# The sixth PV group of a block moved ahead of the last maxima and output products on TensorE

## The chip, the cores and the metric

One NeuronCore of one Trainium2 chip runs the whole kernel. The metric is the device time of one execution in microseconds (us), and the lower the better.

## What is computed

x has 4 x 2048 tokens of 512 features, the context 4 x 154 tokens. The reference, cut to what matters:

```
x = x + attn(layernorm(x), ctx)          # 16 heads of 32; q from x, k and v from ctx; softmax; @ Wo.T + bo
w = softmax(layernorm(x) @ W_router.T + b_router);  keep the two largest of 8
x = x + sum_e w[e] * (layernorm(x) @ W_experts[e].T + b_experts[e])
```

## The kernel before

The tokens are cut into 16 blocks of 512. The first 880 us or so are attention, router and the scatter of the rows to the experts; the rest is the experts' products, which the change doesn't touch.

In the attention part every engine runs a list of steps written out by hand, one list for each slot (`pe_slot`, `act_slot`, `dve_slot`, `pool_slot`, `sp_slot`), and in a slot it works on several blocks at once: on TensorE, b is the block whose scores are computed, b-1 the one whose output product runs, b+1 the one whose maxima are found and b+2 the one whose queries are made. An engine takes its steps strictly in the order of its list. Steps of different engines are tied by semaphores: a step waits until the one that makes its data, or frees its bank, has counted.

The steps that matter here, with their lines:

- **MX** (L726, `pe_MX`): exact scores of six (token tile, head) pairs, products 0 to 10 of block b+1. They go in turn to two pairs of PSUM banks. VectorE takes the maxima (`dve_DMX`, L975; product 10 has only four pairs and two reductions, L979 and L980) into `mx_sb`.
- **O** (L746, `pe_O`): output product of block b-1 in twelve pieces of four matmuls, three for each tile of 128 tokens. VectorE adds a finished tile to x (`dve_Oe`, L987) and takes its statistics (L566, then L574 when all four are there).
- **PV** (L815 and L818, `pe_PV`): probabilities times values of block b in eight groups, 30 small matmuls each. VectorE normalises after each pair of groups (L1083, L1085). PV4 and PV5 are the pair of the third group of heads. Both wait for the same counts: the lower halves of the probabilities up to product 7, and the normalisation of the second pair.
- **MT** (L756, `pe_MT`): four transposes of the 64 maxima; waits for all eleven maxima steps. ScalarE scales them into `mT` (`act_MTe`, L933), SyncE moves that into the query tile (L1351), where the next slot's scores (**ST**, L786 and L789) need it.
- **LB** (L851, L852, L854, `pe_LB`): 36 very small matmuls, router logits of block b-1. Its bank is the one of the last O tile, so it waits for VectorE's last L987. VectorE's L1006 and L1012 read it; L1012 also waits for a chain over L574, ScalarE's L580 and GpSimd's L597 to L1195.
- **Q6** and the rest (L708, `pe_Q`): query product of block b+2. Q6 uses MT's bank and waits for L933. Q9, in the next slot, uses LB's bank and waits for L1012.
- GpSimd issues the **scatter** of an earlier block (L1252, `scatter`): eight indirect DMAs a block, in two groups of four (`pool_SC`, `pool_SD`), between its other steps.

O products and LB are in a slot only when b-1 is a block (from the third MT on); the scatters run in twelve of the slots that have them.

Of the kernel before, what the change touches and what calls it, by code (L numbers as in the profile page):

```python
# [110 lines left out]
def build(nc, x, ctxT, wqT, bq, wkT, bk, wvT, bv, woT, bo, weT, be, wrT, br, wo, boc, out):  # L111
# [543 lines left out]
    def emptied(step, s):  # L655

        chain = HOLDERS[BANK[step]]
        at = [n for n, _ in chain].index(step)
        for back in range(1, len(chain) + 1):
            name, off = chain[at - back]  # L660
            b = s + (off - (back > at))
            if b.here():
                kind = name.rstrip("0123456789")
                signal, n = EMPTIED[kind]
                if kind == name:
                    return signal, b.at(n, n)
                i = int(name[len(kind):])
                if kind == "ST" and i in PLD:
                    return pldd, b.at(ND, PLD.index(i) + 1)
                return signal, b.at(n, (i // 3 if kind in "QO" else i) + 1)  # L670
        return None
# [9 lines left out]
    def split3(k):  # L681
        return ((0, 0, k), (1, 0, k), (0, 1, k))
# [10 lines left out]
    def pe_Q(e, b, i, s):  # L693

        G, part = i // 3, i % 3
        bank = BANK[f"Q{3 * G}"]
        if b.first and i == 0:
            pe_value(e, 2)
            e.wait_ge(p_bk, 5)
        if i == 0:  # L700
            e.wait_ge(t1e, b.at(4, 4))
        if part == 0:
            if free := emptied(f"Q{i}", s):
                e.wait_ge(*free)
        seqs = [t for k in range(KC) for t in split3(k)]
        for n in range(4 * part, 4 * part + 4):
            wp, xp, k = seqs[n]
            m = e.matmul(W[:, bank, :], wq_s[:, wp, k, G * P:(G + 1) * P], xnT[xp][:, k, :], start=(n == 0), stop=(n == 11))  # L708
        if part == 2:
            m.then_inc(qp, 1)  # L710
        if b.first and i == 11:
            pe_value(e, 3)
            pe_value(e, B)
# [18 lines left out]
    def pe_O(e, b, i, s):  # L732

        j, part = i // 3, i % 3
        bank = BANK[f"O{3 * j}"]
        if b.first and i == 0:
            e.wait_ge(p_bk, 6)
        if i == 0:
            e.wait_ge(ate, b.at(4, 4))
        if part == 0:  # L740
            if free := emptied(f"O{i}", s):
                e.wait_ge(*free)
        seqs = [t for k in range(KC) for t in split3(k)]
        for n in range(4 * part, 4 * part + 4):
            ap, wp, k = seqs[n]
            m = e.matmul(W[:, bank, :], aT[ap][:, k, j * P:(j + 1) * P], wo_s[:, wp, k, :], start=(n == 0), stop=(n == 11))  # L746
        if part == 2:
            m.then_inc(op_, 1)
# [44 lines left out]
    def pe_PV(e, b, w):  # L793

        p, G, q = b.par, w // 2, w % 2
        upto = (5 * G + 4) // 2 + 1
        e.wait_ge(pldp, b.at(NP, sum(n < upto for n in PLP)))
        if any(n < upto for n in PLD):
            e.wait_ge(pldd, b.at(ND, sum(n < upto for n in PLD)))
        if b.first and w == 0:  # L800
            e.wait_ge(p_v, 1)
            e.wait_ge(p_vr0, 64)
        elif w == 0:
            e.wait_ge(ld_v[p], b.half(32, 32))
        if b.first and w == 0:
            e.wait_ge(p_rx, 5)
        if w > 1 or b.past(1):
            e.wait_ge(nmd, b.at(4, G))
        for jj in range(2):
            j = 2 * q + jj  # L810
            tok = slice(j * P, (j + 1) * P)
            o = PVp[:, q, jj * 256:jj * 256 + 132]

            for n, (pp, vv) in enumerate(((0, 0), (0, 1), (1, 0))):
                e.matmul(o, Pst[pp][:, (5 * G + 4) % 10, tok], Vr[p][:, vv, G, :], start=(n == 0), stop=(n == 2))  # L815
            for g in range(4):
                for pp, vv in ((0, 0), (0, 1), (1, 0)):
                    m = e.matmul(o[:, g * 33:(g + 1) * 33], Pst[pp][:, (5 * G + g) % 10, tok], Vm[p][:, 4 * G + g, vv, :],  # L818
                                 start=False, stop=True, skip_group_check=True)
        m.then_inc(pvt, 1)  # L820

    def pe_AT(e, b, G, s):
        e.wait_ge(nmd, b.at(4, G + 1))
        pe_T(e, f"AT{G}", b, s, lambda j, k: att[:, j, 4 * k:4 * k + 4, :].rearrange("p h d -> p (h d)"), G, atp)
# [528 lines left out]
    def pe_slot(e, s):  # L1353
        bm2, bm1, b, bp1, bp2 = s + (-2), s + (-1), s, s + 1, s + 2
        on_bm2, on_bm1, on_b, on_bp1, on_bp2 = bm2.here(), bm1.here(), b.here(), bp1.here(), bp2.here()
        if on_bp1:
            pe_Q(e, bp1, 8, s)
        if on_b:
            pe_ST(e, b, 0, s)
            pe_ST(e, b, 1, s)  # L1360
        if on_bm1:
            pe_PV(e, bm1, 6)
        if on_b:
            pe_ST(e, b, 2, s)
        if on_bp1:
            pe_Q(e, bp1, 9, s)
            pe_Q(e, bp1, 10, s)
            pe_Q(e, bp1, 11, s)
        if on_bm1:
            pe_AT(e, bm1, 0, s)  # L1370
            pe_PV(e, bm1, 7)
        if on_b:
            pe_ST(e, b, 3, s)
        if on_bm1:
            pe_AT(e, bm1, 1, s)
        if on_b:
            pe_ST(e, b, 4, s)
        if on_bp1:
            pe_LA(e, bp1, s)
        if on_bm1:  # L1380
            pe_AT(e, bm1, 2, s)
            pe_AT(e, bm1, 3, s)
        if on_b:
            pe_ST(e, b, 5, s)
            pe_PV(e, b, 0)
            pe_PV(e, b, 1)
        if on_bp2:
            pe_XT(e, bp2, 0, s)
        if on_bm1:
            pe_O(e, bm1, 0, s)  # L1390
            pe_O(e, bm1, 1, s)
        if on_b:
            pe_ST(e, b, 6, s)
        if on_bm1:
            pe_O(e, bm1, 2, s)
        if on_bm2 and not bm2.last:
            pe_R(e, bm2, s)
        if on_b:
            pe_ST(e, b, 7, s)
            pe_PV(e, b, 2)  # L1400
        if on_bp2:
            pe_XT(e, bp2, 1, s)
            pe_XT(e, bp2, 2, s)
        if on_b:
            pe_PV(e, b, 3)
            pe_ST(e, b, 8, s)
            pe_ST(e, b, 9, s)
        if on_bp2:
            pe_XT(e, bp2, 3, s)
        if on_bm1 and not bm1.last:  # L1410
            pe_O(e, bm1, 3, s)
            pe_O(e, bm1, 4, s)
            pe_O(e, bm1, 5, s)
        if on_bp2:
            pe_Q(e, bp2, 0, s)
            pe_Q(e, bp2, 1, s)
        if on_bp1:
            pe_MX(e, bp1, 0, s)
        if on_bp2:
            pe_Q(e, bp2, 2, s)  # L1420
        if on_bp1:
            pe_MX(e, bp1, 1, s)
        if on_bp2:
            pe_Q(e, bp2, 3, s)
        if on_bp1:
            pe_MX(e, bp1, 2, s)
        if on_bp2:
            pe_Q(e, bp2, 4, s)
        if on_bp1:
            pe_MX(e, bp1, 3, s)  # L1430
        if on_bm1 and not bm1.last:
            pe_O(e, bm1, 6, s)
        if on_bp1:
            pe_MX(e, bp1, 4, s)
        if on_bp2:
            pe_Q(e, bp2, 5, s)
        if on_bp1:
            pe_MX(e, bp1, 5, s)
        if on_bm1 and not bm1.last:
            pe_O(e, bm1, 7, s)  # L1440
        if on_bp1:
            pe_MX(e, bp1, 6, s)
        if on_bm1 and not bm1.last:
            pe_O(e, bm1, 8, s)
        if on_bp1:
            pe_MX(e, bp1, 7, s)
        if on_b:
            pe_PV(e, b, 4)
        if on_bp1:
            pe_MX(e, bp1, 8, s)  # L1450
        if on_bm1 and not bm1.last:
            pe_O(e, bm1, 9, s)
        if on_bp1:
            pe_MX(e, bp1, 9, s)
        if on_bm1 and not bm1.last:
            pe_O(e, bm1, 10, s)
        if on_bp1:
            pe_MX(e, bp1, 10, s)
        if on_bm1 and not bm1.last:
            pe_O(e, bm1, 11, s)  # L1460
        if on_b:
            pe_PV(e, b, 5)
        if on_bp1:
            pe_MT(e, bp1, s)
        if on_bm1 and not bm1.last:
            pe_LB(e, bm1, s)
        if on_bp2:
            pe_Q(e, bp2, 6, s)
            pe_Q(e, bp2, 7, s)
# [600 lines left out]
```

## Time and profile before

| | |
|---|---|
| three runs | 1326.05, 1328.01 (median), 1336.47 us |
| profiled execution, its own time | 1329.92 us |
| span in its trace | 1328.2 us |
| TensorE busy | 1213.0 us (91%), 11024 matmuls |
| VectorE, ScalarE, GpSimd busy | 66%, 54%, 56% |
| mean granted TensorE clock | 0.963 of full speed |

The own time of the profiled execution is 1.9 us above the median. Starts in the trace are in us from the first instruction. The end of a matmul is modelled; consecutive matmuls overlap, so the distance between starts is what one takes of TensorE's time. A row of the timeline merges equal instructions, and its second number reaches to the end of the last. What stands in brackets is the engine's idle time ahead of the row and what ended it: "issue" is a wait that the profile can't name, "remote" a signal for which it knows no sender at that moment.

### The profile page before, as it was taken

The numbers are of one execution on the slowest core, as the hardware profiler recorded it, in microseconds if no ns is written. First come the engines' busy times: TensorE is split into PE (matmuls) and PEld (weight loads), VectorE is DVE, ScalarE is ACT, GpSimd is POOL, SyncE is SP. The second block draws the span as 40 slices with busy tenths as digits, with TensorE's granted clock in tenths as the row PEclk, the third lists the DMA queues.
The fourth block names the chain that finished last, engine by engine and source line by source line (L and its number), as shares of the span: only waits on it lengthen the run. The fifth ranks groups of instructions, "written<-read, shape, count | busy, mean of one in ns | idle before, by whom it ended". The sixth has DMA issues, their size and how long they took to land.

```text
span 1328.2 us, 36001 instructions
## 1 busy us (share of the span) xinstructions
PE 1213.0 (91%) x11024; PEld 728.8 (55%) x11025; DVE 880.4 (66%) x1933; ACT 720.3 (54%) x1040; POOL 745.2 (56%) x980
## 2 busy tenths in 40 slices
PE   8987999999989989999998987879899999999997
PEld 4445665665655655655666645534355555555554
DVE  4657787878877878878877877435454555555544
ACT  3436875866775775785686572524243333333333
POOL 4013555665775675676676583755644545444445
PEclk9989998999999999999999998879999999999999
DMA  9842654574583583584575364857989989898886
GB/s 265 258 136 66 175 168 139 174 237 135 172 254 141 149 260 140 151 262 143 163 208 165 109 192 167 324 204 166 210 166 188 180 169 192 175 175 164 166 170 124
DMA packets 117114, 239.22 MB, mean 180 GB/s; under 512 B 18439, under 2 KB 24839, under 8 KB 115847
## 3 DMA queue, kind: packets, MB, share of 16 engines
q1 hardware_dynamic: 84535, 161.24, 40.4%
q0 software_dynamic: 29808, 67.73, 25.1%
q10 hardware_dynamic: 2656, 8.68, 1.8%
q8 instruction: 78, 1.28, 0.4%
q14 instruction: 37, 0.30, 0.1%
HBM read 112.00 MB, written 101.40 MB: 161 GB/s over the span
## 4 chain that ended last, share of the span: by engine, by line
PE 66%; ACT 8%; another core or an unknown queue 7%; DMA 6%; issue 5%; DVE 5%; POOL 1%; SPq 1%; POOLq 1%; ACTq 0%; DVEq 0%
PE S L1855 20%; PE W L708 13%; PE W L746 8%; PE W L678 4%; PE PVp L818 4%; DMA out<-xn,to 4%; PE PVp L1845 3%; PE S L786 3%; ACT xn L620 3%; PE S L726 3%; PE PVp L815 2%; DMA xn<-in_wvT 2%; DVE mx_sb L975 1%; PE S L789 1%
## 5 line engine op out<-in xcount | busy, mean ns | idle before, releaser
L1855 PE MATMUL S<-we_s,wq_s 128*128 x1620 | 376.5, 383 | 12.2 <-DVE wq_s L1811 6.7
L1783 POOL DMA_INDIRECT out<-xn,to x135 | 208.9, 1547 | 211.8 <-DMA out<-xn,to 113.0
L1855 PEld LDWEIGHTS S<-we_s,wq_s 128*128 128x128 f16 x1620 | 158.1, 99 | 180.1 <-issue 21.7
L1172 POOL TENSOR_TENSOR we_s<-P_s,we_s 128x1024 f16<-128x1024 f32 x96 | 203.9, 2136 | 60.7 <-ACT we_s L927 60.4
L1794 ACT ACTIVATE wq_s<-PVp 128x512 f16<-128x512 f32 x137 | 81.6, 597 | 272.6 <-PE PVp L1845 252.2
L1252 POOL DMA_INDIRECT dispatched<-xn,idx x128 | 132.8, 1038 | 91.8 <-ACT xn L620 51.8
L975 DVE TENSOR_REDUCE mx_sb<-S 128x6 f32<-128x924 f32 x160 | 171.3, 1112 | 11.2 <-PE S L726 9.1
L708 PE MATMUL W<-we_s,wq_s 128*128 128x512 f16 x512 | 164.8, 400 | 8.7 <-ACT mT L933 5.3
L746 PE MATMUL W<-wo_s,aT_hi 128*128 128x512 f16 x512 | 166.2, 387 | 2.8 <-DVE aT_lo L953 1.6
L1833 DVE SCALAR_TENSOR_TENSOR att<-S,be_s 128x512 f32<-128x512 f32 x135 | 93.4, 692 | 111.3 <-PE S L1855 100.6
L1811 DVE TENSOR_TENSOR wq_s<-PVp,wq_s 128x512 f16<-128x512 f32 x137 | 94.6, 691 | 36.8 <-ACT wq_s L1794 34.7
L818 PE MATMUL PVp<-Vm,we_s 128*128 128x33 f16 x3072 | 118.6, 179 | 0.3 <-issue 0.3
L927 ACT ACTIVATE we_s<-P_s 128x1024 f16<-128x1024 f32 x96 | 101.8, 1060 | 15.2 <-PE PVp L818 12.1
L726 PE MATMUL S<-Kst,we_s 96*128 96x154 f16 x1024 | 99.6, 233 | 10.9 <-DVE mx_sb L975 5.5
L1091 DVE TENSOR_TENSOR we_s<-S,we_s 128x1024 f16<-128x1024 f32 x64 | 78.1, 1220 | 46.2 <-ACT we_s L927 46.1
L818 PEld LDWEIGHTS PVp<-Vm,we_s 128*128 128x128 f16 x3072 | 106.2, 97 | 0.4 <-issue 0.4
L726 PEld LDWEIGHTS S<-Kst,we_s 96*128 96x128 f16 x1024 | 79.1, 99 | 49.4 <-DVE mx_sb L975 8.0
L870 ACT ACTIVATE we_s<-W,bqs 128x512 f16<-128x512 f32 x64 | 44.0, 689 | 113.7 <-PE W L708 113.2
L708 PE MATMUL W<-xnT_lo,wq_s 128*128 128x512 f16 x256 | 101.8, 398 | 1.7 <-issue 1.7
L909 ACT ACTIVATE P_s<-S 128x1024 f32<-128x1024 f32 x96 | 98.2, 1023 | 8.0 <-issue 4.0
L1801 ACT ACTIVATE xn<-att,wt 128x512 f32<-128x512 f32 x135 | 96.3, 714 | 11.2 <-DVE att L1833 5.2
L746 PE MATMUL W<-wo_s,aT_lo 128*128 128x512 f16 x256 | 99.2, 387 | 0.0
(207 smaller groups left out, 2023.5 us busy)
## 6 DMA issues: line engine op xcount, KB each, us to landing
P_s<-dispatched SPq DMA_DIRECT2D x139, 260.5 KB
we_s<-we_s SPq DMA_DIRECT2D x186, 128.0 KB, 6.1
be_s<-in_x SPq DMA_DIRECT2D x16, 1024.0 KB, 9.9
xR_s<-in_x SPq DMA_DIRECT2D x16, 1024.0 KB
out<-xR_s SPq DMA_DIRECT2D x16, 1024.0 KB
wst<-in_weT SPq DMA_DIRECT2D x16, 512.0 KB, 5.7
we_scratch<-wsp SPq DMA_DIRECT2D x16, 512.0 KB, 5.9
Kst<-k_scratch SPq DMA_DIRECT2D x16, 480.0 KB, 5.1
```

The lines of the kernel that those rows point to most:

```text
L708: m = e.matmul(W[:, bank, :], wq_s[:, wp, k, G * P:(G + 1) * P], xnT[xp][:, k, :], start=(n == 0), stop=(n == 11))
L726: m = e.matmul(S[:, 2 * (BANK[f"MX{n}"] - 2) + u % 6 // 3, (u % 3) * C:(u % 3 + 1) * C], Qst[p][0:96, h, j * P:(j + 1) * P], Kst[p][0:96, ...
L746: m = e.matmul(W[:, bank, :], aT[ap][:, k, j * P:(j + 1) * P], wo_s[:, wp, k, :], start=(n == 0), stop=(n == 11))
L818: m = e.matmul(o[:, g * 33:(g + 1) * 33], Pst[pp][:, (5 * G + g) % 10, tok], Vm[p][:, 4 * G + g, vv, :], start=False, stop=True, skip_grou ...
L909: e.activation(P32[i % R32][:, :, :], at, ACT.Exp, scale=1.0 / (SS * ROOT)).then_inc(exd, 1)
L927: e.activation(Pst[0][:, r:r + 2, :], exps(n), ACT.Copy).then_inc(phd, 1)
L975: e.tensor_reduce(mx_sb[:, 6 * n:6 * n + 6].rearrange("p (a k) -> p a k", a=2), S[:, 2 * h:2 * h + 2, 0:3 * C].rearrange("p a (k c) -> p a ...
L1172: e.tensor_tensor(Pst[1][:, r:r + 2, :], exps(n), Pst[0][:, r:r + 2, :], ALU.subtract).then_inc(pldp, 1)
L1252: e.indirect_dma_start(xs_d.ap(), bass.IndirectOffsetOnAxis(ap=idx[p][:, k * NJ + j:k * NJ + j + 1], axis=0), xn2[p][:, j, :], None).then_ ...
L1783: e.indirect_dma_start(out, bass.IndirectOffsetOnAxis(ap=to[u][:, :], axis=0), yw[u % YW], None, bounds_check=N - 1, oob_is_err=False, com ...
L1801: e.activation(yw[u % YW], yb[u % 2], ACT.Copy, scale=wt[u][:, 0:1]).then_inc(ywd, 1)
L1855: m = e.matmul(Yp[:, u % 2, :], gT[u % 2][xp][:, k, :], we_s[:, bass.ds(n * WN + (wp * KC + k) * D, D)], start=(c == 0), stop=(c == 11))
```

## The change

PV5 is issued one O piece, one MX product and one O piece earlier: O10, PV5, MX10, O11, MT in place of O10, MX10, O11, PV5, MT. Nothing is added or removed, and no other engine's list changes.

```
         if on_bm1 and not bm1.last:
             pe_O(e, bm1, 10, s)
+        if on_b:
+            pe_PV(e, b, 5)
         if on_bp1:
             pe_MX(e, bp1, 10, s)
         if on_bm1 and not bm1.last:
             pe_O(e, bm1, 11, s)
-        if on_b:
-            pe_PV(e, b, 5)
         if on_bp1:
             pe_MT(e, bp1, s)
         if on_bm1 and not bm1.last:
             pe_LB(e, bm1, s)
```

## Rows read from the trace of the kernel before

**Rows 1.** Windows: busy time of PE, PEld, DVE, ACT, POOL, clock, DMA, 300 to 400 us

```profile
300.00:400.00 100.00, 92.24 (x1106) 60.00 (x1103) 80.10 (x170) 70.55 (x99) 67.50 (x102) 1.00 0.60 188
```

**Rows 2.** Timeline of PE, 415 to 421 us: start, length, engine, line, idle before

```profile
415.13 0.43 PE L726 MATMUL S<-Kst,we_s 96*128 96x154 f16 x4
...
416.26 0.34 PE L815 MATMUL PVp<-Vr,we_s 128*128 128x132 f16 x3
...
417.22 0.60 PE L756 MATMUL W<-ident,mx_sb 128*16 128x128 f32 x4
417.65 0.25 PE L851 MATMUL W<-wx_s,aT_hi 128*128 128x16 f16 x4
...
420.00 0.17 PE L854 MATMUL W<-wx_s,aT_lo 128*128 128x8 f16 x1 [0.55 <-issue]
...
420.99 1.03 PE L708 MATMUL W<-we_s,wq_s 128*128 128x512 f16 x2 [0.37 <-ACT mT L933]
```

**Rows 3.** Timeline of DVE, 415 to 419 us

```profile
415.71 0.63 DVE L979 TENSOR_REDUCE mx_sb<-S 128x3 f32<-128x462 f32 x1
416.26 0.31 DVE L980 TENSOR_REDUCE mx_sb<-S 128x1 f32<-128x154 f32 x1
416.48 0.68 DVE L987 SCALAR_TENSOR_TENSOR xR_s<-W,xR_s 128x512 f32<-128x512 f32 x1
...
418.60 0.38 DVE L574 BATCH_NORM_AGGREGATE aggr<-stats 128x2 f32<-128x6 f32 x4 [0.24 <-issue]
```

**Rows 4.** Timeline of ACT, 420 to 421 us

```profile
420.26 0.68 ACT L933 ACTIVATE mT<-W,msh 16x512 f16<-16x512 f32 x1 [6.20 <-remote]
420.84 0.28 ACT L580 ACTIVATE nrm<-aggr,epst 128x4 f32<-128x4 f32 x1
```

**Rows 5.** Timeline of POOL, first scatter beside MT

```profile
414.20 1.08 POOL L1252 DMA_INDIRECT dispatched<-xn,idx  x1 [3.73 <-ACT xn L620]
```

**Rows 6.** Timeline of PE in a slot with LB and no scatter

```profile
173.43 0.43 PE L726 MATMUL S<-Kst,we_s 96*128 96x154 f16 x4
...
175.52 0.60 PE L756 MATMUL W<-ident,mx_sb 128*16 128x128 f32 x4
175.96 0.25 PE L851 MATMUL W<-wx_s,aT_hi 128*128 128x16 f16 x4
...
176.89 0.60 PE L708 MATMUL W<-we_s,wq_s 128*128 128x512 f16 x2
```

**Rows 7.** Timeline of ACT in the same slot

```profile
176.16 0.68 ACT L933 ACTIVATE mT<-W,msh 16x512 f16<-16x512 f32 x1 [6.62 <-PE W L756]
```

**Rows 8.** Line L933: its engine's idle time before it, us, times, by releaser

```profile
  remote: 74.6, 12
  PE W L756: 37.9, 4
```

**Rows 9.** Timeline of POOL: first scatter of the second group, one slot earlier

```profile
375.96 1.08 POOL L1252 DMA_INDIRECT dispatched<-xn,idx  x1 [0.62 <-issue]
```

**Rows 10.** Timeline of PE beside it: PV6, end of ST2, end of Q11

```profile
376.03 0.34 PE L815 MATMUL PVp<-Vr,we_s 128*128 128x132 f16 x3
...
377.39 0.39 PE L786 MATMUL S<-we_s,Kst 97*128 97x512 f16 x1
...
379.99 0.38 PE L708 MATMUL W<-xnT_lo,wq_s 128*128 128x512 f16 x1
```

**Rows 11.** Timeline of ACT beside it: the readers of ST2 and Q11

```profile
380.46 1.02 ACT L909 ACTIVATE P_s<-S 128x1024 f32<-128x1024 f32 x1 [0.77 <-remote]
381.91 0.69 ACT L870 ACTIVATE we_s<-W,bqs 128x512 f16<-128x512 f32 x1 [0.42 <-remote]
```

**Rows 12.** Windows, columns as in Rows 1: behind MT of the shown slot

```profile
420.00:425.00 5.00, 4.63 (x31) 2.06 (x32) 1.80 (x6) 2.48 (x5) 2.08 (x10) 0.66 0.52 194
```

**Rows 13.** Timeline of DVE and of PE, next slot's Q9, a short slot

```profile
327.59 0.69 DVE L1012 SCALAR_TENSOR_TENSOR lg<-lgs,nrm,lgq 128x8 f32<-128x8 f32 x4 [3.16 <-POOL lgq L1195]
...
328.65 0.60 PE L708 MATMUL W<-we_s,wq_s 128*128 128x512 f16 x2
```

More of the change, by code:

```diff
@@ L1456, in pe_slot @@
             pe_O(e, bm1, 10, s)
+        if on_b:
+            pe_PV(e, b, 5)
         if on_bp1:
@@ L1460, in pe_slot @@
             pe_O(e, bm1, 11, s)
-        if on_b:
-            pe_PV(e, b, 5)
         if on_bp1:
```

## Prediction

> **What bounds the kernel now.** I read the windows of the attention part first: in a steady stretch of 100 us TensorE is busy 92.24, VectorE 80.10, ScalarE 70.55 [rows 1]. So a slot, which is some 48 us, is bounded by TensorE, and what counts is its idle time. Then the timeline of TensorE around the place of the change. In the shown slot it runs without a gap through MX10 (415.13), O11, PV5 (416.26), MT (417.22) and the start of LB (417.65), then sits idle in pieces that end at 420.00, named "issue", and again until Q6 at 420.99, which waits for ScalarE's L933 [rows 2]. From the start of MT to Q6 it takes 3.77 us for MT and LB; in a slot without the scatter the same work takes 176.89 - 175.52 = 1.37 us [rows 6]. This is the one big hole of a slot, 2.40 us, and the change is made just in front of it.
>
> What makes the hole? L933 needs MT, which ends at 417.82, but starts at 420.26 [rows 2, 4], 2.44 us late. Where no scatter runs it starts 0.04 us behind MT's end (176.12 to 176.16) [rows 6, 7]. The line's own view has the late kind, "remote", 12 times with 74.6 us, the other 4 times [rows 8]. The first scatter of the group begins at 414.20, before PV5 [rows 5]. The same is seen beside the second group of scatters, at another place: the first begins at 375.96 [rows 9], PV6 is issued at 376.03, ST2's last matmul ends at 377.78, Q11's at 380.37 [rows 10]; their readers start at 380.46 and 381.91, both behind an idle ScalarE that waited for "remote" [rows 11]. So **beside scatters, signals of TensorE reach their readers late after a dense group of small matmuls, and come through at about 4.5 us (380.46 - 375.96) or later behind the first scatter**, while TensorE goes on. If more small matmuls follow at once (PV5, MT, LB are 70), TensorE itself stops as well. That the scatter and the density together do it is read from where it happens; no row shows the mechanism.
>
> By the Trainium skill ("Perfetto Trace Analysis", Tensor Engine Instruction) the end of a matmul in a profile is only estimated, and the signal goes out when PSUM has acknowledged the data. By that alone the small matmuls could simply be slower than drawn, everywhere, and the change would move no time at all; the 0.04 us of the slot without scatter speaks against it.
>
> **The change part by part.** (1) *PV5's own work*: the same 30 matmuls, 417.22 - 416.26 = 0.96 us of TensorE wherever they stand [rows 2]; no instruction is added. PV5 waits for the counts that PV4 has already waited for, so it can't wait in its new place: cost 0. It passes no DMA and no step of another queue. Its reader, VectorE's L1083, is far down VectorE's list, so being earlier is worth 0.
>
> (2) *MX10 and its readers go 0.96 us later.* MX10 ends at 416.52 in place of 415.56. VectorE's two reductions run from 415.71 to 416.57 now, 0.86 us, and L987 follows in 0.59 (to 417.16, it starts 0.09 ahead of the drawn end of L980) [rows 3]. O11 now covers them together with PV5; afterwards O11 alone (0.86) does. Without any late signal: reductions 416.54 to 417.40, MT 0.06 later at 417.46 (now 417.22, +0.24), L987 until 417.99, LB at 418.01 (now 417.65, +0.36). In the two slots with LB and without scatter nothing hides that: there MX10 would end at 173.86 + 0.96 = 174.82, the reductions at 175.70, L987 at 176.29, and Q6 at 176.30 + (176.89 - 175.96) = 177.23 in place of 176.89 [rows 6]. **2 x 0.34 = +0.7 us.** In the earlier slots without LB the reductions are behind VectorE's own queue, 0.
>
> (3) *The twelve slots with scatter.* PV5 now spans 415.13 to 416.09, 0.93 to 1.89 us behind the first scatter, and MX10 follows. That is the situation of PV6 and ST2 (0.07 to 1.82 us behind it) [rows 5, 9, 10]. Upper bound: MX10's signal comes as ST2's did, 4.50 us behind the first scatter, at 418.70. Then the reductions end at 419.56, MT is 419.62 to 420.22, L933 starts at 420.26, exactly as now, because the late signal only sits in front of MT and no longer behind it; L987 ends at 420.15, LB takes 420.17 to 421.10, and with it Q6 at 421.10 in place of 420.99: +0.11. One step better: TensorE's restart in LB at 420.00 lies 0.55 + 0.17 = 0.72 behind the one before [rows 2], and if signals come through in such steps, MX10's may come at 418.00; MT is done at 419.5, LB goes 419.5 to 420.4, Q6 between 420.4 and 420.99: -0.3 in the middle. **12 x 0.11 = +1.3, or 12 x -0.3 = -3.6 us.**
>
> (4) *What is late next.* L987 would end at 420.15, 2.99 later, and everything of VectorE behind it. L574 ends at 418.98 now and ScalarE takes it at 420.84 only, because L933 is ahead of it in its list [rows 3, 4]; with +2.99 it is there at 421.97, and L1012, which hangs on it by way of GpSimd, is 1.1 later. L1012 is done 0.37 before Q9 (328.28, 328.65) in the five short slots (those whose Q6 to Q8 aren't slowed or stopped), so Q9 waits 0.75 there [rows 13]: **5 x 0.75 = +3.8 us** with the later signal; with the earlier one (0.7 less) next to nothing. In the other seven the slack is over 1 us.
>
> Sum with the late signal: 0.7 + 1.3 + 3.8 = +5.8 us; with the earlier one: 0.7 - 3.6 = -2.9 us. The rows of ST2 are nearest to the first, but MX10 is smaller and PV5 begins later beside the scatter than PV6 did, so I take the middle, +1.5. From the profiled execution's own time that is 1329.9 + 1.5 = 1331.4, and less the 1.9 by which it lies above the median, 1329.5; I say **1330 us**, with a range of its own from 1322 to 1338.
>
> **Rivals.** (A) *The hole closes.* The 70 small matmuls are no longer in one piece. If TensorE's traffic is not yet slowed so soon behind the first scatter, and fewer matmuls at once are below what makes it stop, then the values of (2) hold: MT 417.46 to 418.06, L933 at 418.10, Q6 behind LB at 418.94, 2.05 us earlier in each of twelve slots, -24.6 us. The clock would gain as well: behind the hole TensorE runs at half clock in the shown slot (mean 0.66 over five us, about 3.4 us at 1.2 GHz in place of 2.4, or 1.7 us lost) [rows 12], and by the same view in five slots in all, -8.5 us. Together 1298; with half of the hole left 1313. I take 1306. For it: the density is the one thing that PV5, MT and LB share with PV6. Against it: PV6 stood alone and still made its followers late [rows 10, 11].
>
> (B) *A wait in place of a wait, and half clock behind every one.* In (3) TensorE stands idle from 417.22 to 419.62 in one piece, just before MT, where now it has pieces with small matmuls between. If that brings the half clock in all twelve slots, seven more than now, it costs 7 x 1.7 = 12 us on top of the late sum: 1328 + 5.8 + 12 = 1346. The point from which it decides is whether MX10's signal is late at all: if it isn't, the wait is the 0.24 us of (2), and there is none of this. The Trainium skill ("TensorE: Matmul & The Clock Gate", What's actually happening) has a clock gate that goes by how busy the array was and has only the two levels; it speaks against this change in so far as the idle time is gathered in one place, and the half clock behind the hole agrees.
>
> (C) *The change does nothing*, since the hole ends at a fixed time behind the scatter whatever stands in it. That is the forecast's middle and within its range.
>
> **How the numbers follow.** Forecast with (C) 0.60, A 0.27, B 0.13. One per cent, 13 us, is what a measurement of this kernel can tell from no change. A lies below 1314.7 for the most part: faster 0.22. B lies above 1341.3 for the most part: slower 0.10. The rest is 0.68. The range has to reach into A and B: 1304 to 1342, leaving out the lower third of A and most of B's upper half.
>
> **What would show it.** Right: in the slot of 417 us MT starts 2 us or more later than O11 ends, idle by VectorE's L980, L933 still starts about 6 us behind the first scatter, LB runs without "issue" pieces, and Q6 comes within 0.5 us of its place. In the slots without scatter MT is 0.2 and LB 0.3 us later. A would show L933 0.04 us behind MT with Q6 two us sooner; B, half clock in more windows behind MT. Wrong would be, most of all, that dense groups close to the first scatter are not held up, since all of (3) hangs on one neighbouring place.

## The result, and the profile after

The kernel with PV5 in front of MX10 and O11 took 1363.08 us (median of 4 runs, 1358.62 to 1367.85) against 1331.63 us of the kernel before in its 4 runs: **ratio 1.0251, 95% interval 1.0209 to 1.0293**, 2.5% slower. (Ratio and interval are those on record; the quotient of the two medians is 1.0236.) A second measurement (e12 below) gave 1.0215 [1.0174, 1.0257]. The forecast of 1330 us and its range, 1304 to 1342, are missed on the slow side. The profiled execution took 1358.62 us, its span is 1356.9 us, its mean granted clock 0.947 (before: 1329.92, 1328.2, 0.963).

The page's line of busy times and its line of the clock:

```profile
PE 1227.4 (90%) x11024; PEld 731.2 (54%) x11025; DVE 880.4 (65%) x1933; ACT 724.0 (53%) x1040; POOL 746.0 (55%) x980
...
PEclk9989999988988989999989888898999999999999
```

Windows of the changed kernel: the stretch of [rows 1], the whole run of slots, and from MT to ST0 in the slot shown below. Columns as in [rows 1]:

```profile
300.00:400.00 100.00, 90.34 (x987) 57.10 (x986) 74.54 (x153) 62.95 (x88) 59.46 (x95) 0.90 0.49 161
220.00:780.00 560.00, 509.67 (x5855) 324.26 (x5856) 421.60 (x874) 370.31 (x507) 354.06 (x539) 0.93 0.55 173
433.18:439.29 6.11, 6.11 (x53) 3.10 (x54) 4.86 (x13) 2.59 (x5) 1.85 (x9) 0.57 0.42 152
```

The long window of the kernel before, for comparison:

```profile
220.00:780.00 560.00, 519.51 (x6246) 337.77 (x6243) 441.69 (x921) 385.06 (x532) 372.38 (x566) 0.98 0.58 183
```

Fewer instructions fit into the same 560 us on every engine (VectorE 874 for 921), and no engine is busier. TensorE's clock has two levels, so a mean of 0.98 is 22 us at 1.2 GHz out of 560, and 0.93 is 78 us. Behind MT of the shown slot it is 0.57.

The slot of [rows 2] in the changed kernel, TensorE's timeline (PV5, MX10, O11's last piece, MT, LB, Q6):

```profile
427.35 0.34 PE L815 MATMUL PVp<-Vr,we_s 128*128 128x132 f16 x3
...
428.31 0.43 PE L726 MATMUL S<-Kst,we_s 96*128 96x154 f16 x4
...
429.22 0.38 PE L746 MATMUL W<-wo_s,aT_hi 128*128 128x512 f16 x1
433.18 1.02 PE L756 MATMUL W<-ident,mx_sb 128*16 128x128 f32 x4 [3.58 <-DVE mx_sb L980]
433.99 0.30 PE L851 MATMUL W<-wx_s,aT_hi 128*128 128x16 f16 x4
...
435.05 1.04 PE L708 MATMUL W<-we_s,wq_s 128*128 128x512 f16 x2
```

VectorE's timeline of the same slot, to be held against [rows 3]:

```profile
432.26 0.64 DVE L979 TENSOR_REDUCE mx_sb<-S 128x3 f32<-128x462 f32 x1 [4.24 <-remote]
432.81 0.31 DVE L980 TENSOR_REDUCE mx_sb<-S 128x1 f32<-128x154 f32 x1
433.04 0.68 DVE L987 SCALAR_TENSOR_TENSOR xR_s<-W,xR_s 128x512 f32<-128x512 f32 x1
```

ScalarE's L933 there, for [rows 4]:

```profile
434.31 0.68 ACT L933 ACTIVATE mT<-W,msh 16x512 f16<-16x512 f32 x1 [8.03 <-PE W L756]
```

GpSimd's first scatter there, for [rows 5]:

```profile
426.42 1.08 POOL L1252 DMA_INDIRECT dispatched<-xn,idx  x1 [3.71 <-ACT xn L620]
```

PV5 makes MX10's signal late, as the prediction's step (3) had it. MX10 ends at 428.74, yet its reader L979 can't start before 432.26, 3.5 us later. MT (TensorE) has to wait 3.58 us for the reductions. In return L933 starts 0.11 us behind MT's end (434.20), where it was 2.44 us late before [rows 2, 4], and LB runs without an "issue" piece. The late signal has moved from MT to MX10. But it comes 432.26 - 426.42 = 5.84 us behind the first scatter, not 4.50. The line views say the same of all slots. For MT (L756), idle time before it and who waited for it:

```profile
  DVE mx_sb L980: 75.2, 26
...
  ACT mT L933: 126.4, 16
```

The "remote" of [rows 8] is gone from L933; all its 16 waits are for MT itself.

**Where the time went.** Take a slot from the last matmul of MX9 to the next one (414.20 to 463.48 in the slot of [rows 2], 49.28 us). The twelve slots with scatter grew from 49.52 to 52.55 us in the mean: 12 x 3.03 = +36.3. The slots ahead of them and the part behind them are 7.6 us shorter in this execution, which leaves +28.7 of span. Of the 3.03, 1.40 us lie between MX9 and Q6 (6.75 to 8.15), 0.79 between Q6 and ST0 (half clock), 0.84 in the rest. In seven of the twelve MX10's signal came about 5.8 us behind the first scatter, in one 5.1, in four about 4.4. Two slots have LB and no scatter beside it. In the first, MX9 to Q6 takes 0.56 us more (predicted 0.34); the last has no Q6, and MX9 to ST0 takes 0.25 more there.

So two things stand side by side, 2.2 to 3.6 us of TensorE waiting in one piece with half clock behind it, and a VectorE that is 4 us later. By its bookkeeping the first alone could be the cause: over the twelve slots (217.07 to 811.34, now 215.52 to 846.09) the mean clock fell from 0.97 to 0.92, which is some 60 us more at half clock, or 30 us of TensorE's time, of the 36.3. Whether it is has to be tried. The waits of VectorE between 220 and 780 us, largest first, in the changed kernel (total us, times, longest):

```profile
DVE mx_sb L979 <- remote: 41.7, 11, 4.2
DVE xnT_lo L953 <- ACT we_s L862: 20.6, 22, 1.8
DVE we_s L1091 <- ACT we_s L927: 17.5, 17, 1.4
...
DVE lg L1012 <- POOL lgq L1195: 11.5, 8, 1.5
```

and in the kernel before:

```profile
DVE we_s L1091 <- ACT we_s L927: 26.7, 22, 2.9
DVE lg L1012 <- POOL lgq L1195: 24.8, 8, 3.2
DVE xnT_lo L953 <- ACT we_s L862: 18.3, 22, 1.8
```

VectorE idles 20 us more than before in total (560 - 441.69 = 118 us, now 138), with 41.7 of it at a place that had none, and the waits which were its reserve further down (L1091 and L1012 above) have shrunk. Which of the two, TensorE's wait or VectorE's lateness, makes the 33 us is what the last experiments decide.

### The profile page after: what moved, and what is told of

It is laid out like the page before. It is cut to its first block and busy times, and to the rows that moved or that the text cites. A ratio compares the mean times of both kernels' runs of the same rounds, so it can differ in the third digit from the quotient of the medians.

```text
span 1356.9 us, 36001 instructions
## 1 busy us (share of the span) xinstructions
PE 1227.4 (90%) x11024; PEld 731.2 (54%) x11025; DVE 880.4 (65%) x1933; ACT 724.0 (53%) x1040; POOL 746.0 (55%) x980
## 3 DMA queue, kind: packets, MB, share of 16 engines
q0 software_dynamic: 29808, 67.73, 24.6%
## 5 line engine op out<-in xcount | busy, mean ns | idle before, releaser
L708 PE MATMUL W<-we_s,wq_s 128*128 128x512 f16 x512 | 173.2, 418 | 5.2 <-DVE xnT_lo L953 3.4
L746 PE MATMUL W<-wo_s,aT_hi 128*128 128x512 f16 x512 | 163.1, 380 | 3.3 <-DVE aT_lo L953 1.7
L1091 DVE TENSOR_TENSOR we_s<-S,we_s 128x1024 f16<-128x1024 f32 x64 | 78.1, 1221 | 45.4 <-ACT we_s L927 39.1
L597 POOL TENSOR_SCALAR nrm<-aggr 128x4 f32<-128x4 f32 x32 | 7.3, 228 | 180.6 <-ACT nrm L582 180.5
L708 PE MATMUL W<-xnT_lo,wq_s 128*128 128x512 f16 x256 | 105.3, 411 | 0.4 <-issue 0.4
```

## The experiments

Ratios are to the kernel before, measured on the same chip, with their 95% intervals; they are those on record, and the quotient of two medians can differ from them by up to 0.003. "A to Q6" is from MX9's last matmul to Q6, a mean over the twelve slots worked out from the timelines (before 6.75, changed 8.15).

**e1: the change, with the scatters later.** Does the lateness belong to the scatter or to the dense group?

```diff
+        if on_b:
+            pe_PV(e, b, 5)
         if on_bp1:
             pe_MX(e, bp1, 10, s)
         if on_bm1 and not bm1.last:
             pe_O(e, bm1, 11, s)
-        if on_b:
-            pe_PV(e, b, 5)
...
-        if on_bm1 and bm1.here(NB - 3):
-            pool_SC(e, bm1)
         if on_b and not b.last:
             pool_NC(e, b, 1)
             pool_RQ(e, b)
         if on_bm1 and bm1.here(NB - 3):
+            pool_SC(e, bm1)
             pool_SD(e, bm1)
```

> The changed kernel with the first group of four scatters issued with the second group, behind GpSimd's L1195, so that no scatter runs beside PV5, MX10 and MT. If a signal is late because a dense group of small matmuls runs beside scatters: in all twelve slots L756 starts 0.1 to 0.4 us behind O11's end (changed kernel 2.2 to 3.6), L933 0.04 us behind L756's end, and from PV5's start to Q6 it takes 4.0 us as in the slot of 173 us (changed kernel 6.7 to 7.7). If the order alone does it, without the scatter, L756 stays 2.2 us or more behind O11. The whole time isn't forecast, since eight scatters in a row also hold GpSimd's L1172 of the next slot: 1320 to 1375 us.

Measured: 1387.4 us, ratio 1.0479 [1.0427, 1.0531]; the signs are as expected for scatter and density together, the time is 12 us above the wide range given. TensorE's timeline at the place of the change (MT, LB, Q6); the first scatter of this slot begins only at 442.57:

```profile
435.22 0.60 PE L756 MATMUL W<-ident,mx_sb 128*16 128x128 f32 x4
436.00 0.24 PE L851 MATMUL W<-wx_s,aT_hi 128*128 128x16 f16 x4 [0.18 <-DVE xR_s L987]
...
436.90 0.59 PE L708 MATMUL W<-we_s,wq_s 128*128 128x512 f16 x2
```

Without a scatter beside it, the same order of the same matmuls has no late signal: MT follows O11's end (435.13) within 0.09 us and A to Q6 is 4.96 us. The loss has moved to where the scatters now are, to the small matmuls of LA. Waits of TensorE between 220 and 780 us:

```profile
PE W L838 <- issue: 24.3, 33, 1.2
PE W L836 <- issue: 20.8, 36, 1.3
```

The kernel before has 4.0 us of such waits before L836 in its whole span. Scatter and dense group are both needed. LA has 32 small matmuls a slot, and TensorE stops in them for 4.1 us a slot (49.5 us in the twelve, next to nothing before), which costs more than the hole that was closed.

**e2: MX10 first, then PV5, then O11.** It takes away the lateness of MX10 but leaves a dense group ahead of O11's signal.

```diff
             pe_MX(e, bp1, 10, s)
-        if on_bm1 and not bm1.last:
-            pe_O(e, bm1, 11, s)
         if on_b:
             pe_PV(e, b, 5)
+        if on_bm1 and not bm1.last:
+            pe_O(e, bm1, 11, s)
         if on_bp1:
             pe_MT(e, bp1, s)
```

> O10, MX10, PV5, O11, MT: the change without its step past MX10. If what stands behind PV5 is what comes late: MX10's signal is prompt, L979 starts where it did before the change, MT is issued behind O11 without a wait, but O11's signal is late, so the last L987 and with it LB start some 2.5 to 3.3 us later than before the change; Q6 0.5 to 1 us later than before: 1336 to 1346 us, under half of the change's 31. If PV5 ahead of O11 does nothing and only the reductions matter: 1328 to 1334 us. If any shift of PV5 costs the same: 1363 us.

Measured: 1345.32 us, ratio 1.0172 [1.0123, 1.0220]. The signals came as expected and the time lies within 1336 to 1346, but it is 21.5 us above the kernel before on the same chip (1323.79), not under half of the change's loss. TensorE's timeline, MT and LB:

```profile
423.82 0.60 PE L756 MATMUL W<-ident,mx_sb 128*16 128x128 f32 x4
427.40 0.24 PE L851 MATMUL W<-wx_s,aT_hi 128*128 128x16 f16 x4 [2.99 <-DVE xR_s L987]
```

and VectorE's:

```profile
422.31 0.63 DVE L979 TENSOR_REDUCE mx_sb<-S 128x3 f32<-128x462 f32 x1
...
426.56 0.69 DVE L987 SCALAR_TENSOR_TENSOR xR_s<-W,xR_s 128x512 f32<-128x512 f32 x1 [3.40 <-remote]
```

MT is issued without a wait, and most of the loss is still there. What is late is again the first signal behind PV5, here O11's to L987, and with it VectorE.

**e3: the changed kernel with the wait filled.** Twelve products that nobody reads stand in front of MT, so that the clock isn't lost.

```diff
+    def pe_fill(e, s):
...
+        for n in range(FILLS):
+            e.matmul(W[:, bank, :], wq_s[:, 0, n % KC, 0:P], wo_s[:, 0, n % KC, :], start=True, stop=True)
...
+        if on_bp1 and on_bm1 and not bm1.last:
+            pe_fill(e, s)
         if on_bp1:
             pe_MT(e, bp1, s)
```

> The changed kernel with twelve 128x512 matmuls (2.6 us), whose result nobody reads, into MT's bank between O11 and MT, in the slots with O. They fit into the wait of 2.2 to 3.6 us in front of MT, and only keep TensorE busy. If half clock behind an idle stretch is a part of the loss by itself: Q6 to ST0 goes from 3.9 to 4.9 back to 2.6 to 3.0 us in most slots, and the time falls by 10 to 20 us to 1343 to 1353. In the slots without scatter they cost 2.2 us each. If the clock is only a sign and not a cost, or 24 more instructions make the late signal later still: 1360 to 1375.

Measured: 1359.85 us, ratio 1.0275 [1.0219, 1.0332]. The clock came back as expected, the time did not fall to 1343 to 1353; it lies at the lower edge of the rival's range. The window of the run of slots:

```profile
220.00:780.00 560.00, 527.36 (x6096) 339.53 (x6093) 427.65 (x881) 373.57 (x513) 355.32 (x541) 0.97 0.55 174
```

Q6 to ST0 fell from 4.38 to 2.75 us, but the time did not fall. The twelve products also cost 2.0 and 2.3 us in the two slots without scatter, where nothing was idle, so I left the question open here and took it up in e11.

**e4: only half of PV5 moved.** How does the lateness depend on the number of small matmuls?

```diff
+        if on_b:
+            pe_PV(e, b, 5, (0,))
         if on_bp1:
             pe_MX(e, bp1, 10, s)
         if on_bm1 and not bm1.last:
             pe_O(e, bm1, 11, s)
         if on_b:
-            pe_PV(e, b, 5)
+            pe_PV(e, b, 5, (1,))
```

> The changed kernel with PV5's second half (15 of 30 matmuls) moved back behind O11. If the delay grows with how many small matmuls stand in front of the signal: MX10's signal comes 1 to 2 us earlier than in the changed kernel, MT starts 1 to 2 us earlier, 1340 to 1355 us. If any small group there is held until the scatters are over: MT where it is in the changed kernel, 1360 to 1366 us.

Measured: 1318.37 us, ratio 0.9974 [0.9940, 1.0009], much better than the 1340 to 1355 us expected. VectorE's timeline of the slot whose first scatter is at 406.63 (MX10 ends at 408.47):

```profile
409.44 0.64 DVE L980 TENSOR_REDUCE mx_sb<-S 128x3 f32<-128x462 f32 x1 [1.22 <-PE S L726]
```

Behind 15 small matmuls MX10's signal is 1.0 us late, 2.8 us behind the first scatter; behind 30 it is 3.5 late, 5.8 behind it. (So in eight and seven of the twelve slots. In the four where the changed kernel has 4.4, the two are 0.3 and 2.2 us late.) So it is no fixed time behind the scatter, as rival C had it. It grows with what stands in front. A to Q6 is 6.60, and the time is that of before: 1 us more for VectorE costs nothing.

**e5: PV5 beside PV4**, where no scatter runs.

```diff
             pe_PV(e, b, 4)
+            pe_PV(e, b, 5)
...
-        if on_b:
-            pe_PV(e, b, 5)
```

> The kernel before with PV5 directly behind PV4, 3.6 us earlier, so that it is over about 0.6 us before the first scatter begins. If only small matmuls beside scatters delay signals: MX10's signal is prompt, MT starts about 0.2 us later than in the kernel before, L933 within 1 us of MT's end (2.4 before), Q6 0.8 to 2 us earlier in each of twelve slots: 8 to 24 us under the kernel before, ratio 0.982 to 0.994. If instead every move of PV5 ahead of MX10 costs, scatter or not: 1.01 to 1.025.

Measured: 1320.87 us, ratio 0.9941 [0.9914, 0.9968], at the slow edge of what was expected. MX10's signal is prompt (0.04 us in the mean) and L933 starts 0.06 us behind MT. The hole is closed, A to Q6 is 4.01, 1.78 us less once PV5's own 0.96 is set aside, 21 us in twelve slots; 8 us of it arrive. The slot is as long as before (49.53) in the profile, which is of the slowest of its twelve executions (1326.06 us). The largest waits of TensorE between 220 and 780 us:

```profile
PE W L678 <- DVE lga L999: 15.2, 11, 1.9
PE S L786 <- DMA we_s<-mT: 5.1, 6, 1.8
PE W L708 <- issue: 5.0, 1, 5.0
```

TensorE now waits for VectorE's L999 for 15.2 us (10.9 before), for the transfer behind mT (5.1, before 0.9), and in one stop of 5.0. It is ahead, and VectorE isn't.

**e6: PV5 between Q6 and Q7.** The hole closed, PV5 again in a place of its own.

```diff
             pe_Q(e, bp2, 6, s)
+        if on_b:
+            pe_PV(e, b, 5)
+        if on_bp2:
             pe_Q(e, bp2, 7, s)
```

> The kernel before with PV5 behind Q6, so that MT has no dense group ahead of it and LB none beside it but its own. If the backlog of small matmuls makes the delay: MT starts 0.6 us earlier than in the kernel before, L933 within 0.5 us of MT's end, Q6 1.5 to 2.8 us earlier in the twelve slots with scatter, half clock behind it in fewer slots: ratio 0.975 to 0.990. If the delay is tied to the scatter alone, whatever TensorE does: L933 still about 6.0 us behind the first scatter, ratio 0.998 to 1.003.

Measured: 1328.46 us, ratio 1.0015 [0.9983, 1.0047]. The signals came as expected (L933 0.06 us behind MT, 3.1 us behind the first scatter, so not tied to the scatter alone), the gain didn't. A to Q6 is 4.01, but PV5 itself is stopped now:

```profile
PE PVp L818 <- issue: 10.3, 19, 0.8
```

That is only a part of it: TensorE still reaches ST0 1.45 us sooner behind MX9 than before (8.89 for 10.34), while the slot is 0.18 us shorter (49.34).

**e7: MT in front of PV5.** L933's signal is asked for before the dense group.

```diff
-        if on_b:
-            pe_PV(e, b, 5)
         if on_bp1:
             pe_MT(e, bp1, s)
+        if on_b:
+            pe_PV(e, b, 5)
```

> The kernel before with MT in front of PV5 (O11, MT, PV5, LB). If the backlog does it: MT's own signal is prompt (L933 within 0.5 us of MT's end), but PV5 and LB together are 66 dense matmuls and TensorE still stops inside LB until about 5.8 us behind the first scatter; Q6 comes 0 to 0.5 us earlier than in the kernel before: ratio 0.994 to 1.001. If it is the transposes or MT's late signal that stop it: Q6 2 us earlier, ratio 0.98 to 0.985.

Measured: 1323.66 us, ratio 0.9966 [0.9935, 0.9996], as expected. L933 follows MT at once; LB still stands still (TensorE's timeline):

```profile
416.79 0.17 PE L852 MATMUL W<-cb_r,ones 128*128 128x8 f16 x1 [0.54 <-issue]
417.53 0.25 PE L854 MATMUL W<-wx_s,aT_lo 128*128 128x8 f16 x4 [0.58 <-issue]
```

The two restarts lie 417.53 - 416.79 = 0.74 us apart, the step read from [rows 2] too.

**e8: the halves of PV5 behind Q6 and Q7.**

```diff
+        if on_b:
+            pe_PV(e, b, 5, (0,))
+        if on_bp2:
             pe_Q(e, bp2, 7, s)
+        if on_b:
+            pe_PV(e, b, 5, (1,))
```

> As e6, but PV5's first half behind Q6 and its second behind Q7, four large matmuls between. If density is what counts, a little better than e6 (0 to 4 us) or the same; if it is no better or worse, e6's PV5 was no longer delaying anything.

Measured: 1322.48 us, ratio 0.9964 [0.9935, 0.9994], 6.0 us below e6 where 0 to 4 were expected. The stops in PV5 go from e6's 10.3 to 7.5 us, and TensorE's wait for L999 (here L1000) from 6.3 to 12.4.

**e9: one half beside PV4, one behind Q6.**

```diff
             pe_PV(e, b, 4)
+            pe_PV(e, b, 5, (0,))
...
             pe_Q(e, bp2, 6, s)
+        if on_b:
+            pe_PV(e, b, 5, (1,))
+        if on_bp2:
             pe_Q(e, bp2, 7, s)
```

> The kernel before with PV5's first half behind PV4 (before the scatters begin) and its second behind Q6 (no MT or LB beside it). The hole is closed as in e5, e6 and e8 (Q6 4.0 us behind MX9's last matmul, before 6.8), and what is late next is spread: reductions 0 to 0.2 us later, one half of PV5 beside Q6. If the backlog explains all: ratio 0.990 to 0.996, as e5 or better. If what e5 and e8 lost again is set elsewhere in the slot, it is no better than they: 0.994 to 0.998.

Measured: 1321.54 us, ratio 0.9921 [0.9888, 0.9954], as expected. It has the lowest ratio of this study, though its interval overlaps those of e5, e7 and e8, and is faster than the two kernels by about 10 us and 40 us. The waits of TensorE between 220 and 780 us:

```profile
PE W L678 <- DVE lga L1000: 16.0, 12, 1.7
PE W L708 <- issue: 5.2, 1, 5.2
PE W L852 <- issue: 2.1, 12, 0.2
```

Of the "issue" pieces in LB, 18.7 us before, 2.1 are left. The wait for L999 (here L1000) is 5.1 us more, and a single stop in front of a product of Q is 5.2 us instead of 1.7.

**e10: LB behind Q7, PV5 where it was.**

```diff
-        if on_bm1 and not bm1.last:
-            pe_LB(e, bm1, s)
         if on_bp2:
             pe_Q(e, bp2, 6, s)
             pe_Q(e, bp2, 7, s)
+        if on_bm1 and not bm1.last:
+            pe_LB(e, bm1, s)
```

> The kernel before with LB behind Q7, so that PV5 and MT are followed by Q6's large matmuls and nothing dense. If the hole is the lateness of MT's signal (PV5 stands in front of it), L933 still starts about 6 us behind the first scatter, Q6 stays at its place with TensorE idle for all of it and LB comes on top: ratio 1.004 to 1.012. If it is LB that stops TensorE and so keeps MT's signal back: L933 starts within 0.5 us of MT's end, Q6 2.4 us earlier: ratio 0.975 to 0.992.

Measured: 1344.03 us, ratio 1.0088 [1.0058, 1.0118], as expected. TensorE's timeline behind MT (420.79 to 421.39):

```profile
424.54 1.03 PE L708 MATMUL W<-we_s,wq_s 128*128 128x512 f16 x2 [3.16 <-ACT mT L933]
```

With nothing behind MT its signal is as late as before. The lateness comes from what stands in front of MT, and LB only filled it.

**e11 and e12: the fill where it belongs, and the changed kernel beside it.** Ten products, only in the loop's slots and their neighbours:

```diff
-FILLS = 12
+FILLS = 10
...
-        if on_bp1 and on_bm1 and not bm1.last:
+        if on_bp1 and on_bm1 and bm1.here(NB - 3) and not bm1.last:
             pe_fill(e, s)
```

> The changed kernel with ten products (128 x 512, results written over by MT) in front of MT, in the slots of the loop and its neighbours only, so that the slots without scatter have none. They fill 2.1 us of the idle 2.4 to 3.6 us in front of MT. Nothing of the result changes. Theory (the half clock behind MT costs part of the 33 us, and e3's total stood high because its twelve products also lay where nothing was idle, and reached beyond the wait in the slots where it is 2.2 us): half clock between MT and ST0 in none or few of the twelve slots, Q6 to ST0 at 2.6 to 2.8 us in place of 4.38, total 8 to 15 us below the changed kernel, ratio to the kernel before 1.014 to 1.020. Rival (what the clock gives back is taken by the next waits, whatever the fill): total as the changed kernel, ratio 1.023 to 1.029.

> The changed kernel itself, beside e11 on the same chip, as its measure. Both theories: ratio to the kernel before 1.021 to 1.029; MX10's signal 5.8 us behind the first scatter in about eight of the twelve slots and 4.4 in the others, half clock behind MT in all twelve.

Measured: e11 1358.26 us, ratio 1.0285 [1.0253, 1.0318]; e12, the changed kernel, 1349.47 us, ratio 1.0215 [1.0174, 1.0257]. e11's theory (1.014 to 1.020) is missed and its rival (1.023 to 1.029) met; e12's ratio is as expected, but it has half clock behind MT in nine of the twelve slots and not in all. Against what the expectation says, the fills stand in 14 slots, the two without scatter among them. The filled slot from MT to ST0, and the run of slots, in e11's windows:

```profile
426.12:430.30 4.18, 4.10 (x53) 2.38 (x54) 3.91 (x11) 2.44 (x5) 0.77 (x4) 1.00 0.24 91
220.00:780.00 560.00, 526.01 (x6094) 336.71 (x6093) 429.85 (x883) 373.33 (x513) 356.12 (x542) 0.97 0.55 174
```

At full clock this stretch takes 4.18 us, not 6.11. Over the 560 us the half clock falls from 67 us (e12's mean is 0.94) to 34. And the kernel isn't faster for it; it is 0.7% slower, 1.0285 against 1.0215.

That whole time overstates it. The fills in the two slots without scatter make up some 3 us, and behind the twelve slots there is a wait that e12, the changed kernel and the kernel before don't have (e3 has it too), with VectorE idle for 8.51 us in front of it for GpSimd's L1257; whether the fills bring it about was not tried. TensorE's timeline:

```profile
872.25 1.46 PE L795 MATMUL S<-we_s,Kst 97*128 97x512 f16 x3 [7.66 <-DVE we_s L1100]
```

So the slots are the better measure. In the twelve slots TensorE reaches ST0 after 11.05 us instead of 12.11, and the next MX9 after 51.55 instead of 51.82: of the 1.06 us that are won 0.79 are lost again in the same slot, and 0.27, or 3.2 us in twelve slots, are kept. The slot is still 2.03 us longer than in the kernel before. Where the 0.79 goes the waits say; e11 first:

```profile
PE W L679 <- DVE lga L1008: 14.9, 11, 1.8
...
PE W L709 <- DVE lg L1021: 4.1, 8, 0.7
```

and the same two in e12:

```profile
PE W L678 <- DVE lga L999: 9.4, 11, 1.7
...
PE W L708 <- DVE lg L1012: 1.1, 2, 0.7
```

TensorE, sooner at its next steps, waits there for VectorE. Most of the half clock that was taken away lay in time that TensorE had to spare.

**e13 and e14: VectorE alone made later, in the kernel before.** Six or two statistics instructions into a tile that nobody reads; TensorE's list is untouched. They stand behind O11's L988 (the kernel before's L987) and one more statistics instruction, so L988 itself and LB are on time, and all of VectorE's list from there on is later, L575 (L574) included.

```diff
             dve_Oe(e, bm2, 3)
             dve_SN(e, bm2, 2)
+        if on_bm2 and bm2.here(NB - 3) and not bm2.last:
+            for k in range(6):
+                e.bn_stats(dump[:, k, :], wq_s[:, 0, 0, :])
```

> The kernel before, with six statistics instructions of VectorE (128 x 512, into a tile that nobody reads) behind the statistics that follow O11's L987, in the slots of the loop and their neighbours. TensorE's order and signals are as before; nothing of the result changes. At the 0.60 us that one of L566 takes beside the next, VectorE's list is 3.6 us later from there on, about as much as the changed kernel's late signal makes it. Theory (the loss is VectorE's list being 4 us later, of which about 1.6 us a slot are absorbed and the rest is passed on, whatever TensorE's clock does): a slot 1.8 to 2.3 us longer, ratio to the kernel before 1.016 to 1.026, at a granted clock near that of before. Rival (VectorE has 10 us of idle time in a slot and absorbs it; the loss was TensorE's own wait and half clock): ratio 0.998 to 1.006.

> The same with two such instructions, 1.2 us. Theory (the slack comes first, the loss only beyond it): a slot 0 to 0.3 us longer, ratio 0.998 to 1.004. Rival (each us costs the same share, 0.55): a slot 0.7 us longer, ratio 1.006 to 1.009.

Measured: e13 1354.58 us, ratio **1.0264 [1.0241, 1.0288]**; e14 1323.26 us, ratio 1.0034 [1.0009, 1.0058]. e14 is as expected; e13's loss is at the upper end of its theory's 1.016 to 1.026, far from the rival's 0.998 to 1.006, but its clock is not near that of before (0.947, before 0.963). VectorE's timeline of e13, O11's L988 and the added group:

```profile
428.05 0.68 DVE L988 SCALAR_TENSOR_TENSOR xR_s<-W,xR_s 128x512 f32<-128x512 f32 x1
...
429.25 3.64 DVE L1640 BATCH_NORM_STATS2 dump<-wq_s 128x6 f32<-128x512 f16 x6
```

and e13's window of the run of slots:

```profile
220.00:780.00 560.00, 518.52 (x6002) 337.12 (x5998) 469.02 (x951) 375.53 (x516) 357.39 (x542) 0.95 0.56 174
```

3.6 us more in VectorE's list costs as much as the whole change, with MT in its old place and A to Q6 even a little shorter (6.59). The mean clock falls to 0.95, 56 us of half clock, though nothing was done to TensorE: here the added half clock is what a late VectorE brings about. The instructions run in 14 slots, so it is 34.8 / 14 = 2.5 us a slot for 3.6; two instructions, 1.2 us, cost 4.5 / 14 = 0.3. By these two about 1 us is free and nearly all beyond it is paid. (In the traces the twelve slots are 1.94 us longer in e13 than in the kernel before and 2.30 longer than in e14, measured on the same chip.)

**All runs by VectorE's place.** The time from MX9's last matmul to the end of O11's L987 (mean of eleven slots from the timelines; for e13 and e14 the added group is put on top), and the ratio:

| kernel | L987 ends, us | later than before | ratio |
|---|---|---|---|
| before | 2.96 | | 1 |
| e5, e6, e7, e8 | 2.96 | 0 | 0.9941, 1.0015, 0.9966, 0.9964 |
| e9 | 2.96 | 0 | 0.9921 |
| e4 | 4.08 | 1.1 | 0.9974 |
| e14 | | 1.2 | 1.0034 |
| e2 | 6.45 | 3.5 | 1.0172 |
| e13 | | 3.6 | 1.0264 |
| e12, the changed kernel | 6.87 | 3.9 | 1.0215 |
| e11, e3 (filled) | 6.88, 6.95 | 3.9, 4.0 | 1.0285, 1.0275 |
| the changed kernel | 7.03 | 4.1 | 1.0251 |
| e10 | 2.96 | 0 | 1.0088 |
| e1 | 3.91 | 0.95 | 1.0479 |

Up to 1.2 us of lateness nothing much happens, at 3.5 us and more it costs 1.7 to 2.9%, whatever TensorE does meanwhile: wait in front of MT (changed), wait in front of LB (e2), multiply what nobody needs (e11), or go on as ever (e13). The last two rows have a loss of another kind, on TensorE: LA stopped by the scatters in e1, and in e10 a wait with nothing in it and LB behind it.

The slots of the same traces, in us, each a mean over the twelve:

| kernel | MX9 to ST0 | whole slot |
|---|---|---|
| before | 10.34 | 49.52 |
| e13 | 10.29 | 51.46 |
| e3 (filled) | 10.71 | 51.65 |
| e11 (filled) | 11.05 | 51.55 |
| e2 | 11.76 | 51.50 |
| e12, the changed kernel | 12.11 | 51.82 |
| the changed kernel | 12.53 | 52.55 |

TensorE reaches ST0 between 0.05 us sooner and 2.2 us later than before, and yet five of these six slots lie within 0.4 us of each other, some 2 us above the kernel before. What the six have in common is VectorE 3.5 to 4.1 us late. The 0.3 us (e12) to 1.0 us (the changed kernel) by which those two lie above 51.5 may be TensorE's own wait and clock.

## Why the prediction was wrong, point by point

- **The mechanism it started from** was right. Signals of TensorE behind a dense group of small matmuls beside scatters are late; moved in front of MX10, PV5 makes MX10's signal late instead of MT's. Of the signs that it named, three are in the trace: MT idle by L980 for over 2 us, LB without "issue", MT 0.25 us later in the slots without scatter (LB 0.6 later there, not 0.3). Two that went by its sizes are not: L933 is 7.9 us behind the first scatter instead of 6, and Q6 1.4 us later in the mean instead of within 0.5. e1 (no scatter, no lateness), e4 (half the group, 1.0 us in place of 3.5) and e10 (nothing behind MT, just as late) show that it is scatter and group together. Its worry that dense groups close to the first scatter are not held up was the wrong worry.
- **Step (1)**, nothing for PV5's own place, held: in e1 the same order has no wait of its own at that place.
- **Step (2)**, the slots with LB and without scatter: 0.56 and 0.25 us instead of 0.34 each, 0.8 us instead of 0.7. Right in kind and in size.
- **Step (3)**, the size of the lateness, was too small. It took ST2's 4.50 us behind the first scatter as the upper bound; measured are 5.8 us in seven slots, 5.1 in one and 4.4 in four. A to Q6 became 1.40 us longer (1.27 in e12) where +0.11 or -0.3 was said. An upper bound had been read off one neighbour, and the forecast then took less than it because PV5 begins later beside the scatter. e4 shows how strongly the lateness goes with the number of matmuls, but PV6 and PV5 have the same 30, so why it is 5.8 here and 4.5 there stays open.
- **Step (4), what is late next, is the step that failed most**. It saw VectorE 2.99 us later and followed a single reader, L1012 before Q9, with a slack of 0.37 us in five slots and over 1 us in seven: +3.8 us in all. Measured by itself (e13), a VectorE list 3.6 us later costs 34.8 us in 14 slots. With some 1 us free a slot as in e14, even the 2.99 us of the prediction would have been about 12 x 2 = 24 us, an estimate; with 3.9 to 4.1 us it is 12 x 3 = 36, and 28 to 33 were measured. The prediction had looked at busy shares (VectorE 80% in [rows 1]) and taken the rest for room. The room is there, but in front of particular waits, and the list behind L987 has only about 1 us of it.
- **Rival B** said slower by a wait in one piece and half clock behind each. Both came: the mean clock behind MT of the shown slot is 0.57, and the time at half clock rose from 22 to 78 us. By the Trainium skill ("TensorE: Matmul & The Clock Gate", What's actually happening) the clock follows how busy the array has been lately; the trace agrees, with 0.57 behind a wait of 3.58 us. But e11 took half of it away and gained 3.2 us in the twelve slots, and in e13 the half clock came by way of VectorE alone, and e5 has more of it than the kernel before (window mean 0.96 for 0.98) and is 0.6% faster, so B's 12 us for the clock isn't what was paid. It was right in its sign and in what it foresaw of the clock, and for the most part wrong in the cause.
- **Rival A**, the hole closes, needs PV5 away from the scatters. Where it did (e5, e6, e8, e9), the 25 us that A promised came to at most 10, since VectorE was then the one to wait for. (A's sum is also off: 1328 + 0.7 - 24.6 - 8.5 is 1296, not 1298.)

**What stays open.** What on the chip holds the signals back. Why e13 costs more than e2 and e12 at about the same lateness; its instructions are in 14 slots rather than 12, keep VectorE busy where the others leave it idle, and stand behind L988, and which of these matters wasn't tried. How much of the 33 us is TensorE's own wait and clock; an estimate from the slots is 0.3 to 1.0 of 2.3 to 3.0 us a slot. Why the signal comes 4.4 us behind the scatter in four slots and 5.8 in most. And which of VectorE's readers passes the lateness on: the waits name L999 and L1012, but no run took one of them away.

## What to carry to other kernels

A stall moved from one engine's signal to another's isn't the same stall: ask which engine's list stands behind the late one. Here 2.4 us late at ScalarE was nearly free (e7 took it away for 0.3%, e5 and e6 took TensorE's hole away with it for 0.6% and for nothing), while 3.5 us late at VectorE cost 2.5%, though Q6 on TensorE came only 1.4 us later. An engine at 80% can still be one of the two that set the pace; its slack is read from the waits that follow in its own list, and best measured by putting a known delay into it alone. And before blaming the clock for a loss, fill the wait in front of it: the clock may only be showing time that was lost already. Then compare the filled stretch itself and not the whole time alone, which here held a wait of 7.66 us somewhere else.

## What the runs showed of the hardware that was not expected

Beside scatters (indirect transfers issued by GpSimd), TensorE's signals behind a group of small matmuls come late, and between the two sizes tried the lateness grew faster than their number: 15 matmuls of 128x33 and 128x132 in front of MX10 made it 1.0 us late (e4), 30 made it 3.5 us late, and without scatters there is none (e1: MT 0.09 us behind O11, with the reductions in between done). When many more follow, TensorE itself stops and starts again in steps of 0.72 to 0.74 us ([rows 2], e7); in LA of e1 its restarts at 449.00, 449.74, 451.19, 452.63, 453.35 and 454.06 lie 0.71 to 0.74 us or twice that apart. In the trace this time is called "remote" at the reader and "issue" at TensorE, and it never names the scatter.
